# A row-scan convolution and a dynamic depthwise block: both ends of the second block rewritten, and matmuls of unused result added while TensorE waits

## The reference

```python
new = cur + relu(row_conv(prev, K))      # 63 steps one after another, four directions
```

```python
pooled = x.mean((2, 3))
dyn = (layernorm(pooled @ w_fc1.T) * ln1_w + ln1_b) @ w_fc2.T   # 5 x 5 taps per image and channel
out = depthwise_conv(x, dyn)                                    # 25 taps
out = channel_layernorm(out) * ln2_w + ln2_b
out = gelu(w_expand @ out)                                      # 64 -> 256 channels
nx  = norm(out over h, w) / (mean over channels + eps)
out = w_shrink @ (gamma * out * nx + beta + out) + x            # 256 -> 64 channels
```

## Time and profile before

| | us |
|---|---|
| median of 3 runs | 870.92 (868.53 to 871.47) |
| the profiled execution | 868.42 |
| span from first to last instruction | 866.5 |
| mean granted TensorE clock | 0.969 |

### The profile page before, as it was taken

The page is one execution under the profiler, slowest core; times in us unless marked ns, Lnnn a source line. Parts: engine busy times, 40 slices in busy tenths (PEclk is TensorE's granted clock), DMA queues, the critical chain, the costliest instruction groups (busy, mean ns, idle before and its releaser), DMA issues. The chain is left out here.

```text
span 866.5 us, 15588 instructions
## 1 busy us (share of the span) xinstructions
PE 782.7 (90%) x5383; PEld 635.1 (73%) x5383; DVE 610.1 (70%) x1111; ACT 413.7 (48%) x501; POOL 455.5 (53%) x443
## 2 busy tenths in 40 slices
PE   5999999999999999999999956778998999998675
PEld 5999999999999999999999945444444444444221
DVE  3666666666656666668888857887989899898712
ACT  5690004776770000000000033499999999989761
POOL 2333333333323333338888826797678787866610
PEclk9999999999999999999999968899999999999987
DMA  6660000000000000000000010222334333433233
GB/s 143 164 155 0 0 0 2 0 0 0 0 1 1 0 0 0 0 1 1 0 0 0 0 48 23 51 55 68 82 77 99 76 79 76 100 97 78 52 76 74
DMA packets 62195, 36.40 MB, mean 42 GB/s; under 512 B 41488, under 2 KB 60112, under 8 KB 62160
## 3 DMA queue, kind: packets, MB, share of 16 engines
q1 hardware_dynamic: 62160, 35.95, 17.6%
HBM read 18.37 MB, written 9.44 MB: 32 GB/s over the span
## 5 line engine op out<-in xcount | busy, mean ns | idle before, releaser
L481 PE MATMUL psum<-line_hi,taps_hi 128*128 128x256 f32 x1270 | 203.0, 292 | 11.9 <-DVE taps_lo L377 8.6
L495 PE MATMUL psum<-line_lo,taps_hi 128*128 128x256 f32 x1270 | 202.7, 291 | 0.8 <-DVE line_lo L430 0.8
L489 PE MATMUL psum<-line_hi,taps_lo 128*128 128x256 f32 x1270 | 202.5, 291 | 0.0
L430 DVE SCALAR_TENSOR_TENSOR line_lo<-psum,rest 128x256 fp32r<-128x256 f32 x254 | 108.1, 426 | 124.3 <-POOL rest L262 114.3
L481 PEld LDWEIGHTS psum<-line_hi,taps_hi 128*128 128x128 f32 x1270 | 177.1, 192 | 13.1 <-issue 9.4
L495 PEld LDWEIGHTS psum<-line_lo,taps_hi 128*128 128x128 f32 x1270 | 176.7, 192 | 2.0 <-DVE line_lo L430 1.8
L489 PEld LDWEIGHTS psum<-line_hi,taps_lo 128*128 128x128 f32 x1270 | 177.1, 192 | 0.0
L262 POOL TENSOR_TENSOR rest<-x,line_hi 128x256 f32<-128x256 f32 x127 | 82.8, 652 | 169.2 <-DVE line_hi L421 169.2
L314 ACT ACTIVATE by_h<-x (+1 forms) x128 | 85.7, 669 | 106.9 <-DVE x L410 105.3
L262 POOL TENSOR_TENSOR rest<-by_h,line_hi 128x256 f32<-128x256 f32 x127 | 91.6, 722 | 83.4 <-DVE line_hi L421 83.4
L731 POOL TENSOR_TENSOR part<-part,prod 128x960 f32<-128x960 f32 (+2 forms) x48 | 108.6, 2263 | 20.4 <-ACT prod L798 15.8
(11 more groups left out here) (126 smaller groups left out, 829.4 us busy)
## 6 DMA issues: line engine op xcount, KB each, us to landing
stage<-in_x_dram SPq DMA_DIRECT2D x32, 256.0 KB, 4.0
rstd_wide<-rstd_dram SPq DMA_DIRECT2D x32, 256.0 KB, 5.4
out_dram<-x SPq DMA_DIRECT2D x32, 256.0 KB, 5.4
crossed<-x SPq DMA_DIRECT2D x16, 256.0 KB, 3.6
crossed<-x SPq DMA_DIRECT2D x16, 240.0 KB, 3.6
rstd_dram<-rstd SPq DMA_DIRECT2D x16, 64.0 KB, 1.5
fc_in<-in_L_conv_w_fc_dram SPq DMA_DIRECT2D x2, 100.0 KB
taps<-in_L_conv_k_td_dram SPq DMA_DIRECT2D x2, 80.0 KB, 3.3
```

The lines of the kernel that those rows point to most:

```text
L430: dve.scalar_tensor_tensor(out=line_lo[:, (slot + 1) % SLOTS, :, part], in0=as_lines(line_ps[slot][:, 0:LINE]), scalar=0.0, in1=as_lines(r ...
L481: mm = pe.matmul(line_ps[slot][:, 0:LINE], taps_hi[:, s, d, :], line_hi[:, slot, :, d:d + WP], start=(d == 0), stop=(d == OFFSETS - 1))
L489: pe.matmul(line_ps[slot][:, 0:LINE], taps_lo[:, s, d, :], line_hi[:, slot, :, d:d + WP], start=False, stop=False, skip_group_check=True)
L495: mm = pe.matmul(line_ps[slot][:, 0:LINE], taps_hi[:, s, d, :], line_lo[:, slot, :, d:d + WP], start=False, stop=(d == OFFSETS - 1), skip_ ...
```

## The change

In the prologue TensorE does the `fc1` product first. The wait of ScalarE on `pads` moves ahead of its copies. TensorE gets 4 matmuls (after the weights) and 12 (after the taps) whose result, in bank 3, is never read; the real convolution overwrites it. `dyn_hi` gets a semaphore of its own, so that the first convolution can begin without `dyn_lo`. VectorE takes the taps of unit 0 chunk by chunk.

At the end the slots stop at 15 and the rest is written out. The last unit's `rstd` isn't sent through DRAM: GpSimd makes selection matrices from the identity (`make_spread`), TensorE multiplies `rstd` by them (`widen`, banks 2 and 3) and VectorE does the norm from PSUM. Three of the last sums of squares move from ScalarE to VectorE. Expands alternate between two bank sets, shrinks of the last units between several banks, and the last two units are stored by chunks.

```diff
+            act.wait_ge(pads, 1)
             act.wait_ge(weights_mm, 1)
...
+            def warm():
+                pe.matmul(conv_ps[0:C, 3, :], x_hi[:, 0, 0, 2:2 + W], x_hi[:, 0, 0:CROWS, 2:2 + W], start=True, stop=True)
...
+            pe.wait_ge(xhi_ready, 1)
+            for _ in range(4):
+                warm()
             pe.wait_ge(hid_ready, 1)
...
             mm.then_inc(pool_mm, 1)
+            for _ in range(12):
+                warm()
...
-                    if u % 2 == 0:
+                    if u == 0:
+                        pe.wait_ge(dyn_first, 1)
+                    elif u % 2 == 0:
                         pe.wait_ge(dyn_ready, b + 1)
...
+            def first_chunk():
+
+                dve.wait_ge(conv_done, 1)
+                dve.wait_ge(crossed_loaded[0], 32)
+                for i in range(N_DVE):
+                    src, rows, cols, weight = place(0, *DVE_TAPS[i])
+                    here = slice(rows.start, CROWS)
+                    dst = inner[:, 0, here, :] if i == N_DVE - 1 else acc[:, 0, here, cols]
+                    link(dve.scalar_tensor_tensor(out=dst, in0=src[:, 0:CROWS - rows.start, :], scalar=weight,
+                                                  in1=acc[:, 0, here, cols], op0=ALU.mult, op1=ALU.add))
...
+            def make_spread():
+
+                pool.wait_ge(part_step, PART_STEPS * UNITS)
+                for k in range(SUBS):
+                    row = kept["ident"][:, :].rearrange("p (g h k a) -> p g h k a", g=4, k=SUBS, a=1)[:, :, 0:2, k, :]
+                    pool.tensor_copy(spread[:, :, k, :].rearrange("p g (h c) -> p g h c", c=C),
+                                     row.to_broadcast([P, 4, 2, C])).then_inc(spread_made, 1)
...
+            def widen(c):
+                if c == 0:
+                    pe.wait_ge(rstd_ready, UNITS)
+                    pe.wait_ge(spread_made, SUBS)
+                    pe.wait_ge(tap_step, N_DVE * UNITS)
+                for g in range(2):
+                    for k in range(SUBS):
+                        at = (g * SUBS + k) * STAT_COLS
+                        mm = pe.matmul(psum[:, 2 + c, at:at + STAT_COLS], spread[:, 2 * c + g, k, :], rstd[:, LAST % 2, :],
+                                       start=True, stop=True)
+                mm.then_inc(wide_done, 1)
...
+            def norm(c):
+                dve.wait_ge(wide_done, c + 1)
+                dve.tensor_tensor(normed[:, LAST % 2, c * COLS:(c + 1) * COLS],
+                                  inner[:, LAST % INNERS, c * CROWS:(c + 1) * CROWS, :].rearrange("p j w -> p (j w)"),
+                                  psum[:, 2 + c, :], ALU.mult).then_inc(normed_ready, 1)
+
+            def add_squares(u, m):
...
+                dve.tensor_tensor_reduce(dump[:, :].rearrange("p (a n) -> p a n", a=2), grown, grown, 1.0, 0.0,
+                                         ALU.mult, ALU.add, energy[:, m, u % 2:u % 2 + 1]).then_inc(energy_ready, 1)
...
             def out_bank(k):
-            return out_ps if k < 4 * (B - 1) else psum[:, 4 + k % 4, :]
+
+            if k < 2 * (LAST - 3):
+                return out_ps
+            return psum[:, (6, 7, 6, 7, 4, 5, 0, 1)[k - 2 * (LAST - 3)], :]
...
-            sp.wait_ge(stored, 32 * UNITS)
+            for u in range(LAST - 4, LAST - 1):
+                store(u)
+            for u in range(LAST - 1, UNITS):
+                for c in range(2):
+                    store_chunk(u, c)
+            sp.wait_ge(stored, 32 * (UNITS + 2))
```

More of the change, by code:

```diff
@@ L641, in block_two @@
         stored = sem("stored")
-        SLOTS_RUN = range(-1, UNITS + 5)
+        SLOTS_RUN = range(-1, UNITS)
         def place(u, kind, col):
@@ L771, in _ @@
                     norm(e)
-                if s < UNITS:
-                    for n in range(1, N_ACT):
-                        add_product(s, n)
+                for n in range(1, N_ACT):
+                    add_product(s, n)
                 if s + 2 < UNITS:
@@ L778, in _ @@
                     make_dyn(s // 2 + 1)
+            make_spread()
+            add_inner(LAST)
+            norm(LAST - 1)
         @block.scalar
@@ L875, in _ @@
                             product(s + 1, p)
+            add_squares(LAST - 2, 1)
+            square(LAST)
+            square_mean(LAST)
+            root(LAST)
+            root_energy(B - 2)
+            for i in range(4):
+                gelu(LAST - 1, i // 2, i % 2)
+                if i == 1:
+                    add_squares(LAST - 1, 0)
+            for i in range(4):
+                gelu(LAST, i // 2, i % 2)
+            root_energy(B - 1)
         @block.vector
@@ L1072, in convolve @@
                     _, col = PE_TAPS[n]
+                    if (u, c, n, part) == (0, 0, 0, 2):
+                        pe.wait_ge(dyn_ready, 1)
                     weight, image = ((dyn_hi, x_hi), (dyn_hi, x_lo), (dyn_lo, x_hi))[part]
@@ L1165, in _ @@
                 at_e(1, 1)
+            shrink(LAST - 4, 0)
+            statistics(LAST)
+            expand(LAST - 1, 0, 0)
+            expand(LAST - 1, 0, 1)
+            shrink(LAST - 4, 1)
+            respond(B - 2)
+            widen(0)
+            widen(1)
+            expand(LAST - 1, 1, 0)
+            shrink(LAST - 3, 0)
+            expand(LAST - 1, 1, 1)
+            shrink(LAST - 3, 1)
+            for m in range(HALVES):
+                for c in range(2):
+                    expand(LAST, m, c)
+            shrink(LAST - 2, 0)
+            shrink(LAST - 2, 1)
+            respond(B - 1)
+            for u in (LAST - 1, LAST):
+                for c in range(2):
+                    shrink(u, c)
 _INS = ['x', 'L0_conv_k_td', 'L0_conv_k_dt', 'L0_conv_k_lr', 'L0_conv_k_rl', 'L1_conv_w_fc1', 'L1_conv_ln1_w',
```

77 lines of the change are left out of this document (58 added, 19 removed).

## The result

| | us |
|---|---|
| before, median of 4 runs | 870.33 (868.53 to 871.47) |
| changed, median of 4 runs | 859.96 (859.67 to 860.78) |
| ratio | 0.9881, 95% interval 0.9867 to 0.9895 |
| profiled execution, before and changed | 868.42 and 859.87 |
| its span; mean granted clock | 866.5 and 857.9; 0.969 and 0.974 |

The account below looks back on a forecast made before the run. Three engines nearly full in the steady part, so only prologue and end move: 1.5 + 6.8 + 1.3 + 1.3 = 10.9 us off 868.42 gives 857.5; half of 2.5 added gives 858.8 us, range 853 to 865.

Parts of the forecast that it names:

- the early product: Prologue: `fc1` about 1.2 us earlier buys nothing, as ScalarE's weight copies hold the square root; -0.2 to +0.3 us, taken 0.
- the twelve: Prologue: unused matmuls after L1051 end at 516.2, seven slow, five fast; convolution starts 0.9 us later but at 2.4 GHz.
- the dummies don't lift it: Prologue rival: clock rises as late as before, convolution held until 517.3; 860.2 us, or 862.7 with first chunk slow; chance 0.12.
- the split: Prologue: unit 0 in two chunks starts VectorE at 519.95; eleven more instructions of 0.24 us; `inner` 1.5 us earlier.
- the point that carries: Prologue: a shift in the end of `inner` of unit 0 (538.15 to 536.65) carries into everything later.
- The phase: Whole run: clock phase likely explains part of the spread; half of the 2.5 us between profiled execution and median added.
- End, to the shrinks: End: earlier norm, sums moved to VectorE and hidden table load start the last shrinks at 844.2 instead of 851.03; 6.8 us.
- only 1.2 us of the 6 show up in the first expand: End: norm done six us earlier, but TensorE's queue limits unit 15's first expand to 832.3 instead of 833.5.
- End, shrinks: End: the last shrinks' 32 records take 9.66 us, 7.1 at 2.4 GHz; gain 0 to 2.6 us, taken 1.3.
- End, stores: End: last store moves 128 KB a DMA instead of 256, landing in 2.2 us instead of 3.5; 1.3 gained, bounds 0 and 2.
- Slow squares: End rival: VectorE's fused sum takes two passes, 4.7 us, ending 5.4 later; 864.2 us, chance 0.09.
- slower than before: End rival: sums of squares on VectorE eat all 10.9 us from 6.5 us each; 874.1 us at 8; chance 0.03.

Follow-up runs that it names:

- e5: Changed kernel with 2 and 5 unused matmuls instead of 4 and 12, and the layernorm's square root ahead of ScalarE's copies of the weights: 857.18 us.
- e9: Changed kernel with the square root ahead of ScalarE's copies of the weights and no unused matmuls: 858.05 us.
- e1: Changed kernel without its 4 and 12 unused matmuls: 860.59 us.
- e3: Changed kernel with 7 and 5 unused matmuls instead of 4 and 12: 858.62 us.
- e10: Changed kernel with 3 and 7 unused matmuls instead of 4 and 12, and the square root ahead of ScalarE's copies of the weights: 856.52 us.

## Why the prediction was right, and where it was not

The time is 1.2 us above the forecast and well in the range. The end went as forecast, the prologue didn't, and a correction that was a guess stood between. So the closeness of the number is partly luck: on the profiled pair, on which the sum was made, it forecast 10.9 and 8.55 came, even with 0.53 from the scans that it hadn't counted, and the 1.25 added for the median made up for half of what the prologue left out.

- *Prologue, the early product.* I took 0, between -0.2 and +0.3. It lost time: the weight products behind it took 2.7 us (503.74 to 506.44) where I carried over before's 1.8, since the clock fell during them, and the copies of the weights waited for them. The load ended 5.25 after `pooled`, before 4.24, and L1150 started 7.28 after, before 6.27. That the copies, not the product, were the cover was right: with the root ahead of them, and no unused matmuls in either, the time went from 860.59 to 858.05.
- *Prologue, the twelve.* The failed step: "seven of the twelve run slow and five fast: they end at 516.2". The clock was to rise 3 us after L1150; it rose at 517.0, so all but the last ran slow, and the convolution began at 517.33, the end that I had given to a late clock. 0.4 of the 1.1 us is their later start, the rest their price, 4.9 us from the first of them to the convolution instead of 4.2. The rival "the dummies don't lift it" came true for their price and not for their purpose: all matmuls of the convolution ran at 0.24 us.
- *Prologue, the split.* Sized 2.6, measured 2.84 (0.26 for each further instruction). `inner` of unit 0 was to end at 536.65 and ended at 538.00, 1.14 of it by the start and 0.21 by the split. Counted from `pooled` the gain of 1.5 is a loss of 0.38. By an estimate from the Trainium skill's page VectorE: DVE Perf Modes, section The TRN2 errata, the split would have cost 1.7; the run says more, not less.
- *Prologue, the point that carries.* "The point whose shift carries into everything later" was wrong too, though it cost this forecast nothing, since hardly any shift came about. In e5 2.23 us at unit 0 were 0.25 at unit 15.
- *The phase.* I added half of the 2.5 us between before's profiled execution and its median. The changed kernel's profiled execution, 859.87, is no better than its median of 859.96, so before's alone was a lucky one, and the whole offset belonged in the sum: 868.42 - 10.9 + 2.5 = 860.0. That this meets the 859.96 is in part chance, since the 10.9 didn't come in the pair. By the medians the change gains 10.4, close to the 10.9: the prologue gives about 2 over many runs, where 1.5 was forecast, though it goes with a higher mean clock and not, as I had argued, with an earlier `inner`. The mean clock of each run would have told me so; I knew only the profiled one's.
- *End, to the shrinks.* 6.8 forecast, 6.52 measured. "Up to `rstd` nothing moves" was off: `rstd` came 8.59 after `inner` of unit 15, before 8.02, with the clock at 0.50 from 813.9 to 817.4, before from 815.3 to 818.7. From `rstd` on the gain was 7.1. Unit 15's expands were to start at 832.3 and started at 833.01; the sums were 2.29 plus 0.08 of readout, forecast 2.3; the reduction was to come at 842.0, from a unit 15 that ended at the same moment (815.46 after, 815.29 before), and came at 842.39. The spreading products were 2.03, forecast 1.9. Right for the right reasons, but one: "only 1.2 us of the 6 show up in the first expand" holds only while nothing else moves. Without the change of the norm it is some 4 us, as the run through DRAM shows; I had not seen that the norm on GpSimd would now meet VectorE's sums of squares, nor that a wait of 3.9 us on TensorE would cost clock.
- *End, shrinks.* 1.3 forecast, 0.91 measured (9.66 to 8.75). The clock was at 0.50 from 844.7 to 848.1, before for some 5 of the 9.66 us. This term was mis-sized within its bounds of 0 to 2.6.
- *End, stores.* 1.3 forecast, 1.34 measured, and 1.33 when undone. The 128 KB stores landed in 2.5 us, where I had put 2.2, so the landing itself explains 1.0 of it. By an estimate from the Trainium skill's page DMA: Bandwidth & Descriptors, section Anatomy of one DMA, it would have been 0.3; the page gives its figures for DMAs that GpSimd issues, and these are issued by SyncE.

Slow squares, and slower than before, were ruled out by 2.29 us a sum.

## What to carry to other kernels

Matmuls of unused result stand in TensorE's queue like real ones: let them end before the operand that the next real one waits for (seven and five: 858.62 us), and first try to bring that operand earlier, which here gave as much without any of them (858.05 us, by a square root moved ahead of three copies). Don't count on a shift at the start to reach the end: look whether a later wait takes it back. Price each edit also by taking it out of the finished kernel: the norm's, worth 1.2 us by the old order, was worth 4 in the new one. And hold a profiled execution's mean clock against that of the timed runs before it is made the base of a sum.

## What the runs showed that I had not expected

- The clock fell soon after the scans and stayed at 0.50 for 13.7 us in the profiled executions of before, the changed kernel, the root first with none, with 2 and 5 and with 3 and 7, whether the convolution had begun 3.7 us before the rise (e9) or after it. It stayed for 17.1 us without unused matmuls (e1) and for 6.8 us with 7 and 5 (e3). What chose between them stays open: e3 was the only one in which TensorE had no wait before the rise, but e5 and e10 each had two timed runs at 0.978 beside others at 0.971, with the same code. The Trainium skill's page TensorE: Matmul & The Clock Gate, section What's actually happening, says that the count of slow matmuls at a start varies from run to run of the same kernel. The one kernel profiled twice, the changed one, doesn't show it at the start (13.7 us both times), but its next low stretch lasted 6.8 us in one execution and 10.2 in the other.
- A GpSimd multiplication of two SBUF operands that starts inside a VectorE operation with two SBUF operands ended 2.21 us after that operation, 3.66 us after its own start.
- VectorE's fused multiply and sum of 2048 fp32 elements takes 2.29 us and 0.08 for the readout; ScalarE's takes 1.91 and 0.19.
- GpSimd copies 512 elements in 0.58 us (1.17 for two), half of what a two-operand sum of that length would be by the 2.35 for 1024.

The fastest kernels here are those with the root first: 856.52 us with 3 and 7 and 857.18 with 2 and 5, whose intervals overlap, against 859.96 of the changed kernel and 870.33 of before.
